# Two selective-scan stages and two axis-scan stages in one kernel: B's matmul a state ahead, loop bodies of six, columns copied contiguous

## The reference, cut to what matters

```python
# layers 0 and 3: 128 channels, 16 states, sequence of 4096 (layer 0) or 16384 (layer 3)
dt = softplus(dt_low @ dt_proj_w.T + dt_proj_b)
def step(h, t):
    h = h * exp(dt_t * A) + dt_t * B_t * xc_t          # B_t, C_t: 16 values a token
    return h, sum(h * C_t, axis=state)
y = (ys + xc * D) * silu(z)                            # then the output projection
# layer 3 alone: projection, layer norm over channels, silu, + residual

# layer 1: sequences of 64 (one column or one row), 192 channels, 96 states
dA = delta * A; dB_u = delta * u * B
c = flip(exp(min(cumsum(flip(shifted dA)), 15)))
x = cumsum(dB_u * c) / (c + 1e-6)
y = sum(x * C, axis=state) + u * D                     # * silu(res), projections, batch norm
```

## Time and profile before

| | us |
|---|---|
| median of 3 runs | 18784.03 (18776.6 to 18786.46) |
| the profiled execution | 18776.8 |
| its span | 18775.0 |
| first sequence stage, about | 1,275 |
| axis stage, columns, about | 7,750 |
| axis stage, rows, about | 7,800 |
| last sequence stage, about | 1,335 |
| busy share PE / DVE / ACT / POOL | 85% / 93% / 75% / 84% |

### The profile page before, as it was taken

The page is one execution under the profiler, slowest core; times in us unless marked ns, Lnnn a source line. Parts: engine busy times, 40 slices in busy tenths (PEclk is TensorE's granted clock), DMA queues, the critical chain, the costliest instruction groups (busy, mean ns, idle before and its releaser), DMA issues. The chain is left out here.

```text
span 18775.0 us, 290434 instructions
## 1 busy us (share of the span) xinstructions
PE 16032.8 (85%) x60184; PEld 8231.0 (44%) x60280; DVE 17441.2 (93%) x48286; ACT 14038.2 (75%) x18466; POOL 15715.6 (84%) x10826
## 2 busy tenths in 40 slices
PE   5777888888888888888878888888888888887777
PEld 2333444444444444444444444444444444443232
DVE  3888999999999999999999999999999999997788
ACT  4666777777777777777777777777777777773577
POOL 2666888888889888889889999999999999996566
PEclk8998999999999999999999999999999999998899
DMA  1001000000000000000000000000000000000000
GB/s 34 13 15 14 11 11 9 11 11 11 11 11 11 11 9 11 11 11 11 13 11 11 11 11 11 11 11 11 11 10 11 11 11 11 11 11 16 17 13 12
DMA packets 778326, 228.79 MB, mean 12 GB/s; under 512 B 747760, under 2 KB 750476, under 8 KB 776332
## 3 DMA queue, kind: packets, MB, share of 16 engines
q1 hardware_dynamic: 772980, 204.65, 8.4%
q10 hardware_dynamic: 3352, 2.14, 0.1%
HBM read 143.66 MB, written 62.97 MB: 11 GB/s over the span
## 5 line engine op out<-in xcount | busy, mean ns | idle before, releaser
L1267 POOL TENSOR_TENSOR h_sm<-h_sm,h_wr 128x768 f32<-128x768 f32 x2944 | 5395.0, 1833 | 697.0 <-DVE h_wr L1023 610.7
L1267 POOL TENSOR_TENSOR w_sm<-w_sm,w_wr 128x768 f32<-128x768 f32 x2944 | 5394.1, 1832 | 509.3 <-DVE w_wr L1023 411.7
L1435 PE MATMUL w_pz<-w_xr,w_tri 128*128 128x384 f32 x9984 | 4460.9, 529 | 788.3 <-DVE w_wr L1023 627.1
L1435 PE MATMUL h_pz<-h_xr,h_tri 128*128 128x384 f32 x9984 | 4432.7, 527 | 770.8 <-DVE h_wr L1023 608.5
L1023 DVE SCALAR_TENSOR_TENSOR h_wr<-h_pz,h_bct,h_rbuf 128x192 f32<-128x192 f32 x11776 | 4252.8, 408 | 179.1 <-PE h_pz L1435 178.2
L1023 DVE SCALAR_TENSOR_TENSOR w_wr<-w_pz,w_bct,w_rbuf 128x192 f32<-128x192 f32 x11776 | 4242.7, 408 | 100.6 <-PE w_pz L1435 100.1
L997 DVE SCALAR_TENSOR_TENSOR h_xr<-h_cbuf,h_bct,h_pdx 128x192 f32<-128x192 f32 x9984 | 3635.3, 405 | 87.4 <-issue 34.0
L997 DVE SCALAR_TENSOR_TENSOR w_xr<-w_cbuf,w_bct,w_pdx 128x192 f32<-128x192 f32 x9984 | 3634.4, 405 | 86.6 <-issue 33.0
L1138 ACT ACTIVATE h_cbuf<-h_pe_e,h_consts 128x1024 f32<-128x1024 f32 x2304 | 2523.5, 1111 | 1530.6 <-PE h_pe_e L1423 1329.5
L1138 ACT ACTIVATE w_cbuf<-w_pe_e,w_consts 128x1024 f32<-128x1024 f32 x2304 | 2524.0, 1111 | 1484.4 <-PE w_pe_e L1423 1296.9
L1161 ACT ACTIVATE w_rbuf<-w_pe_e,w_consts 128x1024 f32<-128x1024 f32 x2304 | 2474.5, 1112 | 0.0
(11 more groups left out here) (366 smaller groups left out, 19654.6 us busy)
## 6 DMA issues: line engine op xcount, KB each, us to landing
h_lt<-pieces_s SPq DMA_DIRECT2D x512, 96.0 KB, 4.4
w_lt<-pieces_s SPq DMA_DIRECT2D x512, 96.0 KB, 4.3
pieces_s<-h_pieces SPq DMA_DIRECT2D x384, 48.0 KB, 2.1
pieces_s<-w_pieces SPq DMA_DIRECT2D x384, 48.0 KB, 2.1
h_xt<-first_s SPq DMA_DIRECT2D x34, 128.0 KB, 5.7
w_xt<-first_s SPq DMA_DIRECT2D x34, 128.0 KB, 3.2
m_u<-hn_s SPq DMA_DIRECT2D x32, 128.8 KB, 2.7
m_u<-slots_s SPq DMA_DIRECT2D x32, 128.8 KB, 2.6
```

The costliest lines, as they stand in the source:

```text
L1267: tt(sm[:, g], sm[:, g], wr[:, u % 3], ALU.add).then_inc(s_add, 1)
L1435: t.matmul(pz[:, P % 2, 0:2 * DX], tri[:], x, start=True, stop=True).then_inc(s_z, 1)
```

## The change

In `phase_mamba` the tables go. The bank is (i * 16 + n) mod 3, carried on from tile to tile, and every B waits for the scan three before it. TensorE's order becomes: B of state n + 1, C of state n, `add` of state n - 4, and the rest as it was. The B of a tile's state 0 is issued in front of C of state 15 of the tile before, with its wait for the tile's split rows. The loop has five turns of six tiles in place of fifteen of two. In `phase_axis` the loop has ten turns of six passes, and the last three passes stand behind it as straight code. In the columns' stage ScalarE copies the next pass's two columns with their history into a new tile `xs` (128x134), and both projections read `xs`.

```diff
@@ phase_mamba
-        BANK = (0, 1, 2, 0, 1, 2, 0, 1, 2, 0, 1, 2, 0, 1, 2, 1)
-        FREED = (4, 2, 4) + (3,) * 12 + (2,)
+        BANKS = 3
...
-            with eng.Fori(0, TILES // 2 - 1) as m:
-                for k in (1, 2):
-                    yield m * 2 + k, k % 2, True, True
-            yield TILES - 1, 1, True, False
+            with eng.Fori(0, (TILES - 2) // 6) as m:
+                for k in range(1, 7):
+                    yield m * 6 + k, k % 2, k * NS % BANKS, True, True
+            yield TILES - 1, (TILES - 1) % 2, (TILES - 1) * NS % BANKS, True, False
...
-                for i, p, before, behind in tiles(pe):
-                    pe.wait_ge(s_bc, i + 1)
+                def b_rows(i, p, r, n):
+                    if n == 0:
+                        pe.wait_ge(s_bc, i + 1)
+                    pe.wait_ge(s_h, i * NS + n + 1 + UB - BANKS)
+                    t.matmul(pb[:, (r + n) % BANKS, :], sel[:, n, :], bc[:, p], start=True, stop=True).then_inc(s_bb, 1)
+
+                b_rows(0, 0, 0, 0)
+                for i, p, r, before, behind in tiles(pe):
                     for n in range(NS):
                         un = i * NS + n
-                        pe.wait_ge(s_h, un + 1 + UB - FREED[n])
-                        t.matmul(pb[:, BANK[n], :], sel[:, n, :], bc[:, p], start=True, stop=True).then_inc(s_bb, 1)
+                        if n + 1 < NS:
+                            b_rows(i, p, r, n + 1)
+                        elif behind:
+                            b_rows(i + 1, 1 - p, r + NS, 0)
                         pe.wait_ge(s_c, un + 2)
                         t.matmul(pc[:], sel[:, NS + n, :], bc[:, p], start=True, stop=True).then_inc(s_cb, 1)
@@ phase_axis
+        if vertical:
+            xs = sb("xs", [128, 2, HIST + SEQ])
...
+        BODY = 6
+        TURNS = (NT2 - 2) // BODY
...
-            with eng.Fori(0, NT2 // 2 - 1) as m:
-                for k in (1, 2):
-                    yield m * 2 + k, k % 2, m + 1, False, False
-            yield NT2 - 1, 1, 0, False, True
+            with eng.Fori(0, TURNS) as m:
+                for k in range(1, BODY + 1):
+                    yield m * BODY + k, k % 2, m * (BODY // 2) + (k + 1) // 2, False, False
+            for T in range(TURNS * BODY + 1, NT2):
+                yield T, T % 2, (T + 1) // 2, False, T == NT2 - 1
...
+                def columns(F, gates):
+
+                    act.wait_ge(s_xt, (F >> 2) * 32 + 32)
+                    if gates is not None:
+                        act.wait_ge(s_ff, gates)
+                    a.activation(xs[:], xt3[:, :, bass.ds((F & 7) * 2, 2)].rearrange("p h s -> p s h"),
+                                 ACT.Copy).then_inc(s_xs, 1)
...
+                            if ch == 0 and vertical:
+                                columns(F, 4 if first else base + 2)
...
-                    if k == 0:
-                        pe.wait_ge(s_xt, (F >> 2) * 32 + 32)
-                    slot = (F & 7) * 2
                     if vertical:
-                        xin = xt3[:, tap:tap + SEQ, bass.ds(slot, 2)].rearrange("p h s -> p s h")
+                        if k == 0:
+                            pe.wait_ge(s_xs, F + 1)
+                        xin = xs[:, :, tap:tap + SEQ]
```

38 lines of the change are left out of this document (21 added, 17 removed).

## The result

The changed kernel takes 18571.3 us (median of 4 runs, 18565.1 to 18573.7), the kernel before 18785.0 us (4 runs, 18776.6 to 18786.5). The ratio is 0.9887, 95% interval 0.987 to 0.9904: 213.6 us less, where 284 were forecast. The profiled execution has a span of 18571.9 us.

A forecast was written before the change was run, and what follows sets the result against it. VectorE was taken to bound the axis stages; in the sequence stages it waits for several engines in turn. Terms -118 - 128 - 46 - 6 + 14 = -284 us took 18784.0 to 18500 us, range 18430 to 18620.

The forecast's parts named there:

- Step 1: Axis stages: 21 fewer jumps in each, at 2.6 and 3.0 us apiece, price unchanged by body length; -118 us.
- Rival (a): Axis stages: the price of a jump grows with the body, so the 118 us stay; 18618 us, chance 0.09.
- Step 2: Columns' stage: contiguous reads speed up projection matmuls, 2.0 us a pass over 64 passes; -128 us, ScalarE's copy booked at 0.
- (c): Columns' stage: ScalarE's added copy is felt; 18538 us, chance 0.07.
- (e): Columns' stage: the 2.0 us a pass are not the stride's, so half the contiguous-columns gain stays; 18564 us, chance 0.06.
- Step 3, first stage: First sequence stage: issuing B ahead of C saves VectorE 1.5 us a tile over 31 tiles; -46 us.
- Step 4: Sequence stages: longer bodies make 8 jumps cost 2.2 us each, less 20 saved jumps at 0.2 us; +14 us.
- Step 3, last stage: Last sequence stage: early B gains 1.8 us, but a late scan 12 leaves net 0.2 us a tile; -6 us.
- rival (d): Sequence stages: C behind waiting B delays in-order TensorE work, 5.4 us a tile, 335 us; 18887 us, slower, chance 0.02.

The follow-up runs named there:

- e1: Changed kernel with old TensorE order in sequence stages, bodies of 2 passes (columns) and 12 (rows): first stage 1213.1, columns 7497.2, rows 7446.4, last 1252.2 us.
- e8: Changed kernel, x and dt projections ahead of B; place 33 summed twice, columns' bodies 20, rows' memset outside loop: first 1137.8, columns 7420.2, rows 7452.7, last 1278.9 us.
- e2: Changed kernel with two-tile bodies and bank tables back, columns read strided, rows' place 33 summed twice: first 1192.1, columns 7559.4, rows 7435.7, last 1312.6 us.
- e3: Changed kernel with dt projection ahead of B(10), columns' place 33 summed twice, rows' bodies of 30: first 1140.5, columns 7439.0, rows 7437.2, last 1280.3 us.
- e6: Changed kernel with B behind C and addition, dt projection (last: x too) ahead; axis bodies 62, place 33 summed twice: 1187.0, 7518.2, 7518.5, 1259.7 us by stage.
- e11: Changed kernel: C, projections, then B; early decay 12; place 33 summed twice, eight memsets, bodies 62 (columns), 30 (rows): 1117.4, 7425.6, 7410.6, 1215.2 us by stage.
- e4: Changed kernel with C ahead of next B; columns' bodies 30, place 33 summed twice; rows' place 20 twice: first 1174.9, columns 7415.0, rows 7455.5, last 1274.3 us.
- e7: Changed kernel: C, x or dt projection, then B; place 33 summed twice, one memset, bodies 62 (columns), 30 (rows): 1127.1, 7526.3, 7414.6, 1242.4 us by stage.

## Why the prediction was right, and where its steps were off

**Right in sign and size, 71 us too optimistic.** By the stages the sum said -182 us for the columns, -63 for the rows, -39 for the first stage and about +1 for the last (each with its share of the jumps), and it came to -162.4, -46.5, -22.3 and +22.5. Every stage fell short, by 17 to 22 us.

**Step 1, fewer jumps, forecast -118: right.** The excess at the start of the passes fell from 81 to 18 us over columns and from 81 to 23 over rows, -121 us. TensorE's jump still takes 3.6 us with a body three times as long. Rival (a) is out: per jump back the excess was 2.7 us before, 2.0 and 2.5 after, 2.2 with bodies of twelve (e1), 3.6 with bodies of twenty (e8's columns), and 1.2 to 3.0 in the eleven stages with bodies of thirty. The Trainium skill (Runtime: NRT & Kernel Launch, "Instruction fetch mechanics") says that a taken branch to a target outside the current two-page window must first fetch the target page, and makes no difference by the length of the body; these numbers agree. What the prediction didn't see is that a good part of the excess goes with the clock: before, a jump with no low clock behind it cost 1.5 us on average, one with 6.8 us of it 3.4, so that some 70 of the 162 us in both stages came with it. No run changed the one without the other, so how much the clock itself takes stays open. And the forecast's 95 us for the surcharge of the rows' stage were not all jumps: 13 of them were the stalls of 8 passes at the lower clock.

**Step 2, contiguous columns, forecast -128: right in its term, with a cost that the prediction didn't see.** The matmuls take 275 ns, the pass 117.5 us, and e2 gives the 2.0 us back when only the stride returns. The copy takes 426 ns, less than the 602 I had as bound, and is hidden; (c) and (e) are out. Missing was the low clock behind the least busy stretch: 23 us of stalls over columns, where there were none, and 7 us more over rows than before. The prediction gave the freed time no cost, and didn't ask what the engine's idle time brings with it. e2 (rows) and e3 (columns) take the stalls away with matmuls that compute nothing new. In the rows' stage the pass itself is unchanged, and yet 12 passes stalled where 8 did, so chance has a part in the number.

The passes behind the loop, "straight code, as the last one is now", were put at no cost; two of them cost 1.5 us each more at place 52 (e6 and e11 show why), 3 us a stage.

**Step 3, first stage, forecast -46: the tile was right, the sum not.** 36.7 us against the 36.5 forecast. 31 x 1.35 = 42 us came in, but 18 us went again in single tiles that take 0.7 to 2.8 us longer than the median: 12.5 us in tiles beside a jump (term 4 had 7 for them), the rest between. With dt_proj ahead (e8) there are hardly any.

**Step 3, last stage, forecast -6: this is the step that failed.** The prediction had 1.8 us gained in the first half and 1.6 lost in the second. Measured from product 0, scan 4 starts 1.04 us earlier than before (9.95 against 10.99) and scan 12 1.08 us later (31.32 against 30.24), so that between them 2.1 us are lost, of which 0.3 come back by the tile's end. The gain was 1.0 us and not 1.8, the loss 1.8 us, net +0.8 us a tile or +24 us for 31 tiles. The gain was over-priced because the tile's first half hangs on TensorE's row of fp32 projections up to the tanhs; taking B's wait away makes VectorE wait for the decay behind those tanhs (0.86 us ahead of scan 4), and they start 0.4 us later than before (8.06 against 7.69 us).

The loss had the right size and, in the main, the right mechanism: C stands behind a waiting B, and the dt projection behind such a C. But it is another C than the prediction had. C(8) behind B(9), which waits for scan 6, already makes `high` 1.07 us late (18.00 against 16.93), and the softplus is as late (21.68 against 20.59); B(10), ahead of C(9) and the dt projection, waits for nothing. With only the dt projection ahead a tile is 0.3 us shorter (e3), since ScalarE then waits for C(9) instead, and with only C ahead 0.4 (e4). C first and the dt projection right behind it win 1.5 together (e7), but part of that isn't the loss taken back: the projection overtakes the addition too, behind which it stood in the kernel before as well. From the softplus to the decay of state 12 ScalarE has no gap, with two table loads of 1.28 us in the row, so it passes the delay on whole. That is rival (d)'s mechanism at a fifth of its price. Its argument against itself, that the x projection isn't used for two states, held: with x_proj behind or ahead of B(8), `high` starts at 18.00 us in any case (after and e8), or at 17.30 with C first (e4 and e7). The expectation of e7, which made x_proj the cause, was right in the number alone.

**Step 4, longer bodies in the sequence stages, forecast +14: of the right size.** The sequencers of ScalarE, VectorE and GpSimd need 2.6 to 3.1 us from the first stage's first jump to their next row. The tiles beside the four jumps take 12.5 us more than the median in the first stage and 5.8 in the last, 18 us for 18 forecast. The agreement is partly luck: in e8 and e11 the same four jumps of the first stage, as long on ScalarE's sequencer, leave no tile over 0.5 us above the median, so that most of the 12.5 us aren't the jumps' own. TensorE's own jump stayed at 0.2 us on the longer loop. With the old order rotation and long bodies together cost 9.8 us in the first stage (e1) and win 12.2 in the last, where the 1.0 us that 12 of the 31 tiles lost ahead of product 1 is gone.

## What to carry to other kernels

An operation that waits should not stand in an in-order queue ahead of one that doesn't, and one for which nobody is in a hurry not ahead of one that feeds an engine without gaps: issue what others need (C, the dt projection) first, then the early B and the addition. Which of two neighbours goes first was worth 1.5 us a tile on TensorE in the last stage (40.32 to 38.81), and one decay ahead of ScalarE's logarithms another 0.8 (37.97), where the edit itself had lost 0.8. And work that gets faster leaves its engine idle: look at the granted clock of the stretches behind, and behind every jump. A timing that comes out as expected doesn't show the cause either: e7 moved two projections, and only a comparison with e3, e4 and e8 told which one counted.
